# FFN routing: token rows stored during the threshold search and gates alone after it on two queues, count spreads on three queues, softmax sums on GpSimd, and the slots of the first four experts before the rest

## What is computed

```python
xn = xf / rms * norm_weight                       # 4096 tokens x 128
logits = xn @ router_weight.T + router_bias       # 16 experts
probs = jax.nn.softmax(logits, axis=-1)
_, idx = jax.lax.top_k(logits.T, 256)             # each expert takes its 256 best tokens
xe = xn[idx]
h = gelu(xe @ fc1.T + fc1_bias); y = h @ fc2.T + fc2_bias   # per expert, 128 -> 512 -> 128
output = zeros.at[idx].add(y * gate); gate_sums = zeros.at[idx].add(gate)
output = output / gate_sums where a token was taken by anyone
```

## Time and profile before

| | |
|---|---|
| median of 3 runs | 735.89 us (734.93 to 737.31) |
| the profiled execution | 735.69 us, span 733.9 us |
| chain that ended last, share of the span | DVE 27%, POOL 22%, issue 17%, DMA 15%, PE 13%, ACT 4% |
| DVE busy | 461.8 us (63%) |
| POOL busy | 355.6 us (48%) |
| PE busy | 410.8 us (56%) |
| search of `feed(1)`, first to last step | about 552 to 591 us |
| from `cnt_ready` to the first gather, each feed | about 15 us |

### The profile page before, as it was taken

The page is one execution under the profiler, slowest core; times in us unless marked ns, Lnnn a source line. Parts: engine busy times, 40 slices in busy tenths (PEclk is TensorE's granted clock), DMA queues, the critical chain, the costliest instruction groups (busy, mean ns, idle before and its releaser), DMA issues.

```text
span 733.9 us, 7537 instructions
## 1 busy us (share of the span) xinstructions
PE 410.8 (56%) x2130; PEld 273.7 (37%) x2130; DVE 461.8 (63%) x1199; ACT 205.2 (28%) x487; POOL 355.6 (48%) x350
## 2 busy tenths in 40 slices
PE   4887560084231396674057888887753313975650
PEld 4554140072110286664023433433331102965540
DVE  6779999997778322222439899999777783222210
ACT  2575000003440142222064334333234401422210
POOL 5048930002000478887308788888720004688853
PEclk9999886589555599998559899999975555999885
DMA  5950000006002523334700000000060024233322
GB/s 139 364 225 0 0 1 0 0 0 172 0 0 52 136 51 47 45 38 64 201 0 0 1 0 2 0 1 0 1 171 1 0 60 130 40 46 44 45 23 18
DMA packets 49860, 38.91 MB, mean 53 GB/s; under 512 B 8672, under 2 KB 46176, under 8 KB 48544
## 3 DMA queue, kind: packets, MB, share of 16 engines
q1 hardware_dynamic: 36000, 28.30, 12.6%
q0 software_dynamic: 11392, 9.05, 9.3%
q10 hardware_dynamic: 2432, 1.11, 0.6%
HBM read 22.73 MB, written 15.73 MB: 52 GB/s over the span
## 4 chain that ended last, share of the span: by engine, by line
DVE 27%; POOL 22%; issue 17%; DMA 15%; PE 13%; ACT 4%; SPq 1%; DVEq 1%; ACTq 0%; POOLq 0%
DVE arena L1021 10%; POOL tb L501 8%; DMA out<-arena,idx 5%; DMA acc<-arena,idx 5%; POOL acc L455 4%; POOL out L455 4%; POOL arena L442 3%; DVE tk L1026 2%; PE ps L807 2%; DVE arena L1026 2%; PE ps L770 2%; DVE tb L1056 2%; DMA tab<-tb 2%; PE ps L855 2%; POOL arena L497 1%
## 5 line engine op out<-in xcount | busy, mean ns | idle before, releaser
L1021 DVE TENSOR_TENSOR arena<-ps,arena 128x256 f32<-128x256 f32 (+1 forms) x36 | 16.4, 454 | 139.6 <-DMA acc<-arena,idx 59.5
L615 ACT ACTIVATE arena<-ps,b 128x256 f32<-128x256 f32 x128 | 50.1, 474 | 143.7 <-PE ps L907 143.7
L501 POOL TENSOR_TENSOR tb<-arena 128x512 f32<-128x512 f32 x64 | 80.4, 1270 | 17.2 <-DVE arena L1369 17.2
L954 PE MATMUL ps<-xT,arena 128*128 128x512 f32 x128 | 71.7, 654 | 20.7 <-DVE arena L1369 20.6
L907 PE MATMUL ps<-arena,f1w 128*128 128x256 f32 x256 | 73.3, 438 | 17.6 <-DVE arena L1025 12.7
L442 POOL DMA_INDIRECT arena<-tab,idx x64 | 62.6, 978 | 41.5 <-DMA tab<-tb 22.6
L917 PEld LDWEIGHTS ps<-f2w,arena 128*128 128x128 f32 x512 | 64.2, 197 | 4.4 <-issue 2.2
L917 PE MATMUL ps<-f2w,arena 128*128 128x128 f32 x512 | 63.9, 279 | 2.0 <-DVE arena L1025 2.0
L907 PEld LDWEIGHTS ps<-arena,f1w 128*128 128x128 f32 x256 | 53.8, 221 | 27.4 <-DVE arena L1025 14.4
L455 POOL DMA_INDIRECT out<-arena,idx x32 | 50.9, 1590 | 23.5 <-issue 10.5
L271 POOL DMA_DIRECT2D arena<-cntd x4 | 2.7, 687 | 117.3 <-DMA cntd<-arena 117.3
(11 more groups left out here) (230 smaller groups left out, 936.8 us busy)
## 6 DMA issues: line engine op xcount, KB each, us to landing
tab<-tb SPq DMA_DIRECT2D x8, 576.0 KB, 5.7
f1w<-in_f1T SPq DMA_DIRECT2D x4, 1024.0 KB, 12.5
f2w<-in_f2T SPq DMA_DIRECT2D x4, 1024.0 KB, 14.3
acc<-tb SPq DMA_DIRECT2D x8, 256.0 KB, 18.7
arena<-in_f2b SPq DMA_DIRECT2D x2, 1024.0 KB, 6.0
acc<-xs SPq DMA_DIRECT2D x8, 256.0 KB, 6.5
xs<-acc SPq DMA_DIRECT2D x8, 256.0 KB, 5.8
arena<-acc SPq DMA_DIRECT2D x8, 256.0 KB, 5.4
```

The costliest lines, as they stand in the source:

```text
L501: pool.tensor_tensor(QS[:, i, :], ST[:, r, i, :], qn[:, r, :], ALU.mult).then_inc(qs_ready, 1)
L615: last = nc.scalar.activation(hT[:, e % 2, t, :], ps[:, 2 * (e % 2) + t // 2, (t % 2) * CAP:(t % 2 + 1) * CAP], ACT.Gelu, bias=b1[:, e, t: ...
L954: nc.tensor.matmul(ps[:, u % V_BANKS, :], WV[:, i, :, :].rearrange("p h a -> p (h a)"), xT[:, n * GW:(n + 1) * GW], start=True, stop=True) ...
L1021: return nc.vector.tensor_tensor(o, a, b, op)
```

## The change

Six things change in each feed, none in what is computed.

- Rows: the 128 features of all rows of `tb` are stored to `tab[f]` as soon as they are normalised, on SP, ahead of the wait for `cnt_ready`. After the search only the 16 gates of each row are stored (`store_gates`, 64 bytes a row), two DMAs on SP and two on ACT.
- Spreads: three on SP, three on ACT, two on GpSimd, where it was six and two.
- Softmax: GpSimd adds the 16 exponentials of a token in four halving steps after `exped`. DVE takes the reciprocals (`rsum`) in the middle of the tie handling, and GpSimd multiplies (`prob_ready`).
- The gates are written by one DVE instruction in place of four.
- Slots: the experts are split in `FIRST` = 4 and 12. DVE compares for ten experts, finishes `idx` for the first four, compares for the other six, and finishes the rest. The first four use PSUM banks 6 and 7 and a tile of their own, `le16`.
- Waits: the first gather waits for the first part of `idx`, the ninth for the second; `turn(0)` on PE waits for the second part.

```diff
+        NSP = 3
+        NACT = 3
+        def store_gates(queue, f, q):
+            queue.wait_ge(tab_ready, f + 1)
+            queue.dma_start(tab[f][q * 1024:(q + 1) * 1024, D:TW].rearrange("(t p) w -> p t w", p=P), tb[:, 8 * q:8 * q + 8, D:TW]
+                            ).then_inc(tab_stored, 16)
...
+                sp.wait_ge(normed, NORMED[1 + 2 * f] + ND)
+                sp.wait_ge(normed_pool, (NG - ND) * (f + 1))
+                for q in range(4):
+                    sp.dma_start(tab[f][q * 1024:(q + 1) * 1024, 0:D].rearrange("(t p) w -> p t w", p=P), tb[:, 8 * q:8 * q + 8, 0:D]
+                                 ).then_inc(tab_stored, 16)
                 sp.wait_ge(cnt_ready, f + 1)
                 sp.dma_start(cntd[f][:, :], cnt).then_inc(cnt_stored, 16)
                 sp.wait_ge(cnt_stored, 16 * (f + 1))
                 for c in range(NSP):
                     spread_counts(sp, f, c, seg_in)
-                sp.wait_ge(tab_ready, f + 1)
-                for q in range(4):
-                    t = slice(8 * q, 8 * q + 8)
-                    sp.dma_start(tab[f][q * 1024:(q + 1) * 1024, :].rearrange("(t p) w -> p t w", p=P), tb[:, t, :]
-                                 ).then_inc(tab_stored, 16)
+                store_gates(sp, f, 0)
+                store_gates(sp, f, 1)
...
+                pool.wait_ge(exped, f + 1)
+                ex = exs.rearrange("p (t e) -> p t e", e=NE)
+                w = NE // 2
+                G.step(pool.tensor_tensor(exsum[:, :, 0:w], ex[:, :, 0:w], ex[:, :, w:2 * w], ALU.add))
+                while w > 1:
+                    w //= 2
+                    last = pool.tensor_tensor(exsum[:, :, 0:w], exsum[:, :, 0:w], exsum[:, :, w:2 * w], ALU.add)
+                    if w > 1:
+                        G.step(last)
+                last.then_inc(sum_ready, 1)
+                pool.wait_ge(rsum_ready, f + 1)
+                pool.tensor_tensor(ex, ex, rsum.rearrange("p (t e) -> p t e", e=1).to_broadcast([P, NT, NE]), ALU.mult
+                                   ).then_inc(prob_ready, 1)
...
                     if s == 0:
-                        pool.wait_ge(idx_ready, f + 1)
+                        pool.wait_ge(idx_ready, 2 * f + 1)
+                    elif s == 2 * FIRST:
+                        pool.wait_ge(idx_ready, 2 * f + 2)
...
+                act.wait_ge(cnt_stored, 16 * (f + 1))
+                for c in range(NSP, NSP + NACT):
+                    spread_counts(act, f, c, seg_in_act)
+                store_gates(act, f, 2)
+                store_gates(act, f, 3)
                 act.wait_ge(seg_diff, f + 1)
...
-                pe.wait_ge(idx_ready, f + 1)
+                pe.wait_ge(idx_ready, 2 * f + 2)
...
                 V.did(nc.vector.tensor_tensor_scan(cnt, eq, eq, 0.0, ALU.add, ALU.max))
+                dve.wait_ge(sum_ready, f + 1)
+                nc.vector.reciprocal(rsum, exsum[:, :, 0]).then_inc(rsum_ready, 1)
                 dve.wait_ge(totalled, base + NR + 1)
...
-                dve.wait_ge(exped, f + 1)
-                V.step(nc.vector.tensor_reduce(smx, ex, AX.X, ALU.add))
-                V.step(nc.vector.reciprocal(smx, smx))
-                V.step(tt(ex, ex, over(smx), ALU.mult))
+                dve.wait_ge(prob_ready, f + 1)
...
+                onehots(0, FIRST).then_inc(onehot, 1)
+                onehots(FIRST, 10)
+                slots(0, 6, 0, FIRST)
+                onehots(10, NE).then_inc(onehot, 1)
+                slots(1, 4, FIRST, NE)
```

More of the change, by code:

```diff
@@ L875, in feed @@
                 nc.tensor.matmul(ps[:, 3, :], differ[:, :], cs16, start=True, stop=True).then_inc(seg_diff, 1)
-                pe.wait_ge(onehot, f + 1)
+                pe.wait_ge(onehot, 2 * f + 1)
                 pe.wait_ge(cd_ready, f + 1)
                 for h in range(2):
-                    for e in range(NE):
+                    for e in range(FIRST):
+                        last = nc.tensor.matmul(ps[:, 6 + h, e * 32:e * 32 + 32], G16[:, e, h * P:(h + 1) * P],
+                                                cd16[:, e * 32:e * 32 + 32], start=True, stop=True)
+                last.then_inc(slots_ready, 1)
+                pe.wait_ge(onehot, 2 * f + 2)
+                for h in range(2):
+                    for e in range(FIRST, NE):
                         last = nc.tensor.matmul(ps[:, 4 + h, e * 32:e * 32 + 32], G16[:, e, h * P:(h + 1) * P],
@@ L1264, in feed @@
                 V.step(nc.vector.reciprocal(rinv, rinv))
-                for q in range(TPG):
-                    gate = tt(tb[:, q::TPG, D:TW], ex[:, q * NCH:(q + 1) * NCH, :], over(rinv)[:, q * NCH:(q + 1) * NCH, :], ALU.mult)
-                gate.then_inc(tab_ready, 1)
+                tt(tb[:, :, D:TW].rearrange("p (c q) e -> p q c e", q=TPG), ex.rearrange("p (q c) e -> p q c e", q=TPG),
+                   over(rinv).rearrange("p (q c) e -> p q c e", q=TPG), ALU.mult).then_inc(tab_ready, 1)
@@ L1268, in feed @@
                 V.did(nc.vector.memset(cd16.rearrange("p (e t) -> p e t", e=NE)[:, :, 31:32], 1.0))
                 dve.wait_ge(seg_in, 16 * NSP * (f + 1))
-                dve.wait_ge(seg_in_pool, 16 * (NCH - NSP) * (f + 1))
+                dve.wait_ge(seg_in_act, 16 * NACT * (f + 1))
+                dve.wait_ge(seg_in_pool, 16 * (NCH - NSP - NACT) * (f + 1))
                 nc.vector.tensor_copy(cs16, csg).then_inc(seg16, 1)
-                for e in range(NE):
-                    last = ts(G16[:, e, :], srow[:, :], csg[:, 32 * e + 31:32 * e + 32], None, ALU.is_lt)
@@ L1274, in feed @@
-                last.then_inc(onehot, 1)
-                dve.wait_ge(slots_ready, f + 1)
-                lev3 = G16.rearrange("p e s -> p (e s)")[:, 0:2 * NE * 31].rearrange("p (h t) -> p h t", h=2 * NE)
-                for h in range(2):
-                    V.did(ts(lev3[:, h * NE:(h + 1) * NE, :], ps[:, 4 + h, :].rearrange("p (e t) -> p e t", e=NE)[:, :, 0:31],
-                             scol[:, h:h + 1], None, ALU.is_le))
-                V.settle()
-                V.step(nc.vector.tensor_reduce(lesum, lev3, AX.X, ALU.add))
@@ L1282, in feed, with onehots @@
-                col = ps[:, 4:6, :].rearrange("p h (e t) -> p (h e) t", e=NE)[:, :, 31:32]
-                V.step(stt(lesum, col.rearrange("p a t -> p (a t)"), -32.0, lesum, ALU.mult, ALU.add))
-                ts(idx[:, :], lesum, 32.0 * P, None, ALU.add).then_inc(idx_ready, 1)
+                def onehots(e0, e1):
+                    for e in range(e0, e1):
+                        last = ts(G16[:, e, :], srow[:, :], csg[:, 32 * e + 31:32 * e + 32], None, ALU.is_lt)
+                    return last
@@ new lines, in slots @@
+                def slots(part, bank, e0, e1):
+                    ne = e1 - e0
+                    dve.wait_ge(slots_ready, 2 * f + part + 1)
+                    le3 = G16.rearrange("p e s -> p (e s)")[:, 0:2 * ne * 31].rearrange("p (h t) -> p h t", h=2 * ne)
+                    if part == 0:
+                        le3 = le16[:, 0:2 * ne * 31].rearrange("p (h t) -> p h t", h=2 * ne)
+                    for h in range(2):
+                        V.did(ts(le3[:, h * ne:(h + 1) * ne, :], ps[:, bank + h, :].rearrange("p (e t) -> p e t", e=NE)[:, e0:e1, 0:31],
+                                 scol[:, h:h + 1], None, ALU.is_le))
+                    V.settle()
+                    le = lesum[:, 0:2 * ne]
+                    V.step(nc.vector.tensor_reduce(le, le3, AX.X, ALU.add))
+                    col = ps[:, bank:bank + 2, :].rearrange("p h (e t) -> p h e t", e=NE)[:, :, e0:e1, 31]
+                    le = le.rearrange("p (h e) -> p h e", h=2)
+                    V.step(stt(le, col, -32.0, le, ALU.mult, ALU.add))
+                    ts(idx.rearrange("p (h e) -> p h e", h=2)[:, :, e0:e1], le, 32.0 * P, None, ALU.add).then_inc(idx_ready, 1)
```

11 lines of the change are left out of this document (8 added, 3 removed).

## The result

The changed kernel took 731.57 us (median of 8 runs, 727.21 to 733.19), the kernel before 736.84 us (8 runs). The ratio is 0.9916, with a 95% interval of 0.989 to 0.9942, so 5.3 us less. The forecast of 730.5 us, 5.2 us less than the profiled execution before, has the right size. The path to it has two errors of opposite sign that nearly cancel.

The account below looks back on a forecast made before the run. The gate branch was taken to release the gathers, the index branch only just ahead. Late C of 2.5 us against gains of 5.25 in feed(0) and 4.95 in feed(1) gave 735.7 − 5.2 = 730.5 us, range 725.5 to 739.

Parts of the forecast that it names:

- the gate branch: After the search, from softmax and gates to the table's landing; said to release the gathers before, index branch 0.4 us less.
- the index branch: After the search, spreads, conversion, comparisons and slots up to `idx`; complete at 611.98 before, against the table's landing at 612.37.
- The small stores: Gate stores after the search: 13.5 ns per 64-byte packet, table landed at C+8.3, ahead of the first part of `idx`.
- C: Time zero in each feed: the end of DVE's second scan, `cnt_ready`, at the end of the search.
- Rivals 1 and 4: Gate stores: 1, dear packets at 32.2 or 82 ns, 737.7 or 763 us, chance 0.22; 4, about 25 ns, 734.0, 0.13.
- The gathers: After table and first part of `idx`: first gather at C+9.75, gain 5.25 us; transpose at C+14.05, gain 4.95.
- the start-up of 0.4: Before the first gather: 0.4 us, read from 612.37 to 612.79, added after the first part of `idx`.
- The narrow pass: DVE's slots for the first experts: comparisons 0.5 us, reduction 0.4, small steps 0.5; first part of `idx` at C+9.35.
- C late: Ahead of C: reciprocal +0.38, stretched tie operation +1.0, GpSimd sums +1.1; together 2.5 us a feed, bounds 0.4 and 3.3.
- the main case: Whole kernel: 13 to 20 ns a packet, C late by 1.5 to 3.3 us, time 728.5 to 733; chance 0.52.
- The sum: Both feeds: 2.5 − 5.25 = −2.75 in feed(0), 2.5 − 4.95 = −2.45 in feed(1); 730.5 us.
- Rival 2: Before C: GpSimd's work costs DVE nothing, C late by the reciprocal alone, time 726.3 us; chance 0.13.

Follow-up runs that it names:

- e10: Kernel before plus the early slots of four experts alone; rows stored whole after the search, spreads six and two, softmax on DVE: 736.19 us beside 736.93, ratio 0.9992.
- e6: Changed kernel with the slots of all 16 experts in one pass, as before the change: 744.77 us, ratio to the kernel before 1.0021.
- e5: Changed kernel with nothing stored during the search and whole 576-byte rows stored after it on SP and ACT: 742.24 us beside 742.38 of before, ratio 0.9999.
- e1: Changed kernel with the gate stores on SP and ACT waiting until all eight spreads have landed: 731.62 us, ratio to before 0.9911.
- e3: Changed kernel with DVE's reciprocal of the sums moved ahead of DVE's last wait of the search: 729.92 us, ratio to before 0.9902.
- e4: Changed kernel with the softmax sums, reciprocal and multiplication back on DVE after C: 727.87 us, ratio to before 0.9874.
- e11: Changed kernel with the softmax back on DVE, measured again on one chip with the changed kernel: 728.06 us, ratio to before 0.9895.
- e8: Changed kernel with spreads six on SP and two on GpSimd, as before the change: 738.33 us beside 742.38 of before, ratio 0.9933.
- e7: Changed kernel with the softmax back on DVE and spreads four on SP, four on ACT: 733.02 us beside 742.38 of before, ratio 0.987.
- e12: Changed kernel with the softmax back on DVE and spreads four on SP, four on ACT, on the last batch's chip: 725.35 us, ratio to before 0.9843.
- the last batch: Five rounds on one chip: the changed kernel itself (731.32 us, ratio 0.9917), e10, e11 and e12.

## Why the prediction came out

**What bounds it: right, except for the branch that came last.** The two branches ended almost together, and one alone gains nothing. e10 shows it for the early slots, e6 for the early table, e5 for late whole rows. But which of them released the gather I read wrongly. The prediction says that "the gate branch, not the index branch, releases the gathers", since the first gather came 0.4 us behind the table's landing. Where the table surely decides, in both feeds of e1, e5 and e10, the gather starts 0.27 to 0.28 us behind the landing; before, it was 0.62 and 0.42. Where `idx` decides, it starts 0.80 to 0.94 us behind `idx`; before, it was 0.87 and 0.81, and the changed kernel has the same two values. So `idx` released the gathers before, and the table landed 0.35 and 0.15 us earlier than it had to. This is also what e10 gained at the first gather, 0.3 and 0.2 us. The forecast survives, since both branches were shortened.

**The small stores: right.** 16.7 ns a packet and a table at C+8.8 and C+8.9, 0.5 us behind the forecast and ahead of `idx`. Rivals 1 and 4 are out: a packet cost none of their 25, 32 or 82 ns. Whatever the rule of the Trainium skill's page "DMA: Bandwidth & Descriptors", section Specifications, on transfers under 512 B means for other writes, these 64-byte writes cost 16.7 ns where 128-byte reads cost 13.5.

**The gathers: right in kind, 1.4 us too early.** Forecast C+9.75, measured C+11.1. The step that failed is "the last to be issued is GpSimd's second, landing 2.5 us later, so C+5.5": the landing time of GpSimd's spreads was taken from the kernel before, with two queues, and held constant with three. It rose to 3.4 us, and the conversion stayed at C+6.5 to C+6.7 (1.1 us). The other 0.45 us is the start-up of 0.4, taken from the table's landing, which should have been 0.85 from `idx`. The narrow pass itself took 3.75 us from the conversion, forecast 3.85. The transpose was forecast at C+14.05 and came at C+15.2, again the 1.1 us of the spreads. The Trainium skill's page "DMA: Bandwidth & Descriptors", section Issuing engines are not separate DMA queues, says that starting DMAs on several engines saves only the time it takes to start them. The traces agree: the eight spreads were issued in 1.2 us less, and the conversion came no earlier. I quoted it and still moved the landing.

**C late: right in kind, mis-sized.** Forecast 2.5, measured 1.24, below the 1.5 to 3.3 of the main case. The reciprocal cost 0.22 and not 0.38; it starts 0.08 us before the scan in front ends. The tie operation lost 0.68 and not 1.0. GpSimd's multiplication took 1.06 us, not 1.26, and the tie operation, beside it for 0.89 us, ended 0.55 us after it in both feeds, where it takes 0.75 alone. The sums at the search's start cost 0.3 and not 1.1, since only two of DVE's operations were held up.

**The sum.** By feed: late C 1.24 and gather 3.9 earlier gives −2.6 in feed(0); 1.24 and transpose 3.75 earlier gives −2.5 in feed(1). That is −5.1 where I had −5.2; a shorter way from transpose to scatter in feed(1) makes it the 5.5 of the stage marks. Both errors were 1.2 to 1.4 us a feed, with opposite signs. That the kinds were right is the prediction's merit; that the sum came out within 0.1 us is luck. Rival 2 (GpSimd's work costs nothing) is refuted by e3 and e4.

## What to carry to other kernels

Where two branches join at a wait, price both before moving either, and shorten them together: here the early slots alone gave 0.1% or nothing (e10), the early table nothing while `idx` was late (e6), and both gave 1% (e11). Work moved to an idle engine isn't free when both engines work on SBUF operands at the same time: three hidden DVE instructions became a stretch of visible ones, and putting them back was worth 2 to 3 us. Issuing small DMAs on more queues brought the last issue forward by 1.2 us here and the landing by nothing with three queues, 0.3 to 0.4 us with four and four. So take a landing time from traffic of the same density. And take the start-up from the releaser's own end, in a run in which nothing else can be the releaser.

## What the runs showed of the hardware

- DVE and GpSimd: a DVE operation of 128x512 on two SBUF operands took 1.43 us beside a GpSimd multiplication that covered 0.89 us of it, and 0.75 without (e3). The loss of 0.68 is less than the overlap. A DVE counting operation with one tensor operand took 0.75 us with the multiplication beside it and without (e3).
- GpSimd's multiplication with one operand repeated 16 times along each row took 1.06 us for 512 elements. Its multiplications of two full operands of 512 elements took 1.27 us (mean of 64, L532, changed kernel).
- A first indirect gather started 0.80 to 0.94 us after the end of the DVE instruction that released it (20 cases) and 0.27 to 0.28 us after the landing of the DMA that released it (6 cases). The later ones started 0.30 us after the end of the one before.
- 4096 writes of 64 bytes to HBM on two queues cost 16.7 ns of an engine's time each, and 576-byte writes 32.2 ns.
- In feed(1) the way from transpose to first scatter was 11.8 to 12.3 us where TensorE's granted clock rose from 0.50 to 1.00 within 5.7 us of the transpose, and 12.8 to 13.9 us where it rose after 7.1 us or more (ten profiles, without those of e5 to e8).
- On the chip of e5 to e8 PE paused for 1.0 to 2.2 us in feed(0) with no releaser in all four profiles. The kernel before was 0.7% slower there than on the chip of the last batch, and the kernel of e7 and e12 1.1%. That the pauses come from the chip is not shown.
